# An attention and expert-FFN kernel: the work between the first attention and the expert gather is redistributed over the engines, and the expert loop is written out with its row scaling on VectorE alone

## What is computed

```
x = x + L0_xattn(layernorm(x), ctx, ctx)            # 32 heads of 8
h = layernorm(x)                                    # L0 experts: 8 experts, top 2
logits = h @ router_w.T; top 2 of softmax, renormalised
expert(h) = down( up(h) * square(relu(gate(h))) )   # every linear is "bitlinear":
  bitlinear(a, w): a rounded to 127 steps of its row maximum, w to {-1,0,1} of its mean
x = x + sum over the two experts of weight * expert(h)
x = x + L1_xattn(layernorm(x), ctx)                 # 16 heads, rope, latent keys
x = x + L1_ffn(layernorm(x))                        # top 1 of 32 masked ternary matrices
```

## Time and profile before

| what | value |
|---|---|
| median of 3 runs | 449.67 us (447.81 to 506.16) |
| the profiled execution's own time | 448.24 us |
| its span, first to last instruction | 446.1 us, mean granted clock 0.941 |
| busy: PE, DVE, ACT, POOL | 82%, 75%, 48%, 29% of the span |
| share of the chain that ended last: PE, ACT, DVE, issue, DMA | 58%, 14%, 11%, 8%, 5% |

### The profile page before, as it was taken

How to read it: one execution, slowest core, us unless ns; L and a number is a source line. 1 busy time by engine, 2 the same in 40 slices (tenths; PEclk the granted TensorE clock), 3 DMA queues, 4 the chain that set the end, 5 groups by cost and what they waited for, 6 DMA issues and landing times.

```text
span 446.1 us, 10544 instructions
## 1 busy us (share of the span) xinstructions
PE 367.6 (82%) x3670; PEld 254.5 (57%) x3677; DVE 332.6 (75%) x848; ACT 213.0 (48%) x467; POOL 129.9 (29%) x137
## 2 busy tenths in 40 slices
PE   2678878814777779998999999999999989638995
PEld 1466667712444446765457566475574778525884
DVE  6969999897888888598588777886876535673453
ACT  3799998261688888673013121231232221225441
POOL 1110000205466653111293141350430410153334
PEclk9999999755799999999999999999999999858999
DMA  8996850511265551441112112032031101343001
GB/s 289 411 395 241 316 199 3 190 41 38 33 243 174 166 153 50 143 175 40 45 51 95 25 73 95 1 95 95 1 96 53 44 1 60 130 108 94 18 32 37
DMA packets 17182, 50.76 MB, mean 114 GB/s; under 512 B 2104, under 2 KB 6464, under 8 KB 15088
## 3 DMA queue, kind: packets, MB, share of 16 engines
q1 hardware_dynamic: 14272, 42.46, 26.4%
q0 software_dynamic: 2864, 7.68, 5.9%
HBM read 43.44 MB, written 6.69 MB: 112 GB/s over the span
## 4 chain that ended last, share of the span: by engine, by line
PE 58%; ACT 14%; DVE 11%; issue 8%; DMA 5%; SPq 1%; POOL 1%; ACTq 0%; DVEq 0%; POOLq 0%
PE bank L956 17%; PE bank L1170 8%; PE bank L972 6%; PE bank L1044 5%; ACT W L1203 4%; DMA raw<-in_L_ffn_w_dram 3%; PE bank L983 3%; PE bank L815 3%; PE bank L826 2%; PE bank L997 2%; ACT hid L1294 2%; PE bank L833 2%; PE bank L1023 2%; ACT pnat L1189 2%; PE bank L1007 2%
## 5 line engine op out<-in xcount | busy, mean ns | idle before, releaser
L1734 DVE TENSOR_TENSOR roped<-bank,cst 128x512 f32<-128x512 f32 x96 | 61.1, 685 | 29.0 <-PE bank L956 28.0
L608 POOL TENSOR_TENSOR WE<-WE,wT 128x512 f32<-128x512 f32 x32 | 42.2, 1347 | 82.1 <-DMA WE<-_L_ffn_expert_masks_dram 82.1
L956 PE MATMUL bank<-XNT_hi,AW_hi 128*128 128x512 f32 x96 | 41.8, 435 | 0.5 <-DVE XNT_lo L1786 0.5
L1339 ACT ACTIVATE qrT<-bank 128x512 f32<-128x512 f32 x16 | 8.7, 595 | 62.2 <-PE bank L983 62.2
L956 PE MATMUL bank<-XNT_lo,AW_hi 128*128 128x512 f32 x96 | 37.8, 393 | 0.0
L956 PE MATMUL bank<-XNT_hi,AW_lo 128*128 128x512 f32 x96 | 37.6, 391 | 0.0
L1333 ACT ACTIVATE prob<-prob 128x512 f32<-128x512 f32 x16 | 10.1, 632 | 44.3 <-DVE prob L1744 44.3
L972 PE MATMUL bank<-roped,MW 128*64 128x512 f32 x128 | 31.0, 605 | 0.0
L1044 PE MATMUL bank<-VW,ctxT 128*128 128x256 f32 x128 | 30.7, 385 | 0.0
L580 POOL DMA_INDIRECT xg<-x_rows,owner_b x23 | 22.3, 971 | 28.1 <-DVE owner_b L428 14.2
L956 PEld LDWEIGHTS bank<-XNT_hi,AW_hi 128*128 128x128 f32 x96 | 18.0, 187 | 19.9 <-issue 11.4
(11 more groups left out here) (306 smaller groups left out, 874.8 us busy)
## 6 DMA issues: line engine op xcount, KB each, us to landing
raw<-in_L_ffn_w_dram SPq DMA_DIRECT2D x8, 1536.0 KB, 7.8
fold<-in_L_xattn_fold_dram SPq DMA_DIRECT2D x8, 1024.0 KB, 5.9
WE<-_L_ffn_expert_masks_dram SPq DMA_DIRECT2D x8, 1024.0 KB, 5.4
kv<-in_keys_values_dram SPq DMA_DIRECT2D x8, 656.0 KB, 7.6
yg<-y_rows SPq DMA_DIRECT2D x8, 256.0 KB, 4.7
x_tok<-pay SPq DMA_DIRECT2D x8, 256.0 KB, 2.2
X<-in_x_dram SPq DMA_DIRECT2D x4, 256.0 KB, 9.6
x_rows<-xrow SPq DMA_DIRECT2D x1, 516.0 KB, 4.3
```

The source lines that it names most:

```text
L608: pool.tensor_tensor(WE[:, e], WE[:, e], wT[:], ALU.mult).then_inc(WE_ready, 1)
L956: mm = pe.matmul(bank[g][:], a[:, k, c * P:(c + 1) * P], b[:, k, g * 512:(g + 1) * 512], start=k == 0 and i == 0, stop=k == 1 and i == 2)
L1734: ins = dve.tensor_tensor(roped[n][:, r, :].rearrange("p (b s) -> p b s", s=S), src, cst[:, None, at:at + S].to_broadcast([P, 8, S]), ALU. ...
```

## The change

Two groups of edits, both ahead of 182 us. Nothing of stage 4 changes but the semaphore counts that it waits for.

Routing chain. The inverse root goes to POOL as one power; each tile's mean is aggregated as the tile comes (`mean_ready`), and POOL centres rows 0 to 6 into XC during the attention. Row maxima are taken of XC (`row_peaks`) and scaled by the inverse root afterwards. ACT quantises tiles 0 to 3 and POOL tiles 4 to 7, and `xrow` is stored in two halves. The router's statistics and its turning move into the attention (tile 5 and tile 7). The last two tiles are turned singly (`turn_late_x1`), the logits of seven tiles are copied ahead of the last tile's, and ahead of the keys. `at_row` becomes 16 narrow instructions on a bf16 iota; the multiplications of `of_block` go to POOL (tile) and ACT (row).

Expert loop. PE's and DVE's loops are written out. `gate_up` runs four blocks ahead instead of three, `down` one block later. DVE scales every block; ACT no longer scales hidden rows but makes the output scale of each block (`output_scale`, formerly L1667 on DVE).

```diff
-            link(dve.tensor_tensor(R.of_block[:, 0], blk[...], cst[...], ALU.is_equal))
-            for k in range(R.choices):
-                dve.tensor_tensor(R.of_block[:, 1, c], R.of_block[:, 0, c], cst[:, C_TILE...], ALU.mult)
-            dve.tensor_scalar(R.of_block[:, 2], R.of_block[:, 0], cst[:, C_ROW:C_ROW + 1], None, ALU.mult)
-            for k in range(R.choices):
-                dve.tensor_tensor(R.at_row[:, c], lo[:, c, None]..., cst[:, None, C_IOTA...], ALU.is_equal).then_inc(spots_ready, 1)
+            dve.tensor_tensor(R.of_block[:, 0], blk[...], cst[...], ALU.is_equal).then_inc(of_block_ready, 1)
+            for c in range(n):
+                dve.tensor_scalar(R.at_row[:, c], iota_b[:], lo[:, c:c + 1], None, ALU.is_equal).then_inc(spots_ready, 1)
...
 # POOL
-            link(pool.tensor_scalar(less_mean[:], mv[:, :, 0], -1.0, 0.0, ALU.mult, ALU.add))
-            for t in range(NT // 2, NT):
-                pool.tensor_scalar(XN[:, t, :], X[:, t, :], less_mean[:, t:t + 1], rstd[:, t:t + 1], ALU.add, ALU.mult).then_inc(XN_pooled, 1)
-            pool.wait_ge(xrow_stored, 16)
+            for t in range(NT - 1):
+                pool.wait_ge(mean_ready, t + 1)
+                pool.tensor_scalar(XC[:, t, :], X[:, t, :], mv[:, t, 0:1], 1.0, ALU.subtract, ALU.mult).then_inc(rows_pooled, 1)
+            pool.wait_ge(var_ready, 2)
+            pool.tensor_tensor(rstd[:], var[:], minus_half[:], ALU.pow).then_inc(root_ready, 1)
+            pool.wait_ge(xs_ready, 1)
+            for t in range(NT // 2, NT):
+                pool.tensor_scalar(xq32[:, t, :], XC[:, t, :], xs[:, t:t + 1], MAGIC, ALU.mult, ALU.add).then_inc(rows_pooled, 1)
+            pool.wait_ge(of_block_ready, 1)
+            for k in range(2):
+                ins = pool.tensor_tensor(RB.of_block[:, 1, c], RB.of_block[:, 0, c], cst[:, C_TILE...], ALU.mult)
+            ins.then_inc(of_tile_ready, 1)
+            pool.wait_ge(xrow_stored, 32)
...
 # PE, routing
+            turn_x1(2)
             weigh(NT - 1)
+            pe.wait_ge(r_ready, 1)
+            router_logits([0])
             turn_outputs(NT - 1)
-            for h in range(3):
-                router_logits(h)
-            turn_x1(3)
-            router_logits(3)
+            router_logits([1])
+            turn_late_x1(NT - 2)
+            router_logits([2, 3])
+            turn_late_x1(NT - 1)
+            router_logits([4, 5, 6]).then_inc(logits_ready, 1)
+            router_logits([7]).then_inc(logits_ready, 1)
...
 # PE, experts
+            gate_up(3, expert_at(3))
+            for j in range(NBLK):
...
+                turn_hidden(j)
+                if j + 4 < NBLK:
+                    turn_rows(j + 4)
+                if j:
+                    down(j - 1, expert_at(j - 1))
+                if j + 4 < NBLK:
+                    gate_up(j + 4, expert_at(j + 4))
...
 # ACT, experts
                 hidden_rows(j, j % 2)
...
-                if j + 3 < NBLK:
-                    relus(j + 3, (j + 3) % 2)
-                if j % 2 == 0 and j + 1 < NBLK:
-                    scale_hidden(j + 1)
-                outputs(j)
+                output_scale(j)
+                if j:
+                    outputs(j - 1)
+                if j + 4 < NBLK:
+                    relus(j + 4, j % 2)
...
 # DVE, attention and routing
-                if t == NT - 2:
+                link.after(measured)
+                dve.bn_aggr(mv[:, t - 1, :], stats[:, t - 1, :]).then_inc(mean_ready, 1)
+                if t == NT - 3:
                     dve.wait_ge(r_loaded, 16)
                     link(dve.bn_stats(r_stats[:], r_raw[:]))
...
             dve.wait_ge(logits_copied, 1)
+            tops(range(NT - 1))
+            peaks = link.note(dve.tensor_reduce(row_max[:, 3, NT - 1:], XC[:, NT - 1:], AX.X, ALU.max, apply_absolute_value=True))
+            dve.wait_ge(logits_copied, 2)
+            topped = tops([NT - 1])
+            dve.wait_ge(root_ready, 2)
+            scaled = link.note(dve.tensor_tensor(row_max[:, 0, :], row_max[:, 3, :], rstd[:], ALU.mult))
+            top_indices([0, 1])
+            scale = link.note(dve.tensor_scalar(row_max[:, 0, :], row_max[:, 0, :], EPS, 1.0 / QMAX, ALU.max, ALU.mult))
...
 # DVE, experts: one block
+                if j:
+                    scale = link.note(dve.tensor_scalar(was[:, 2:3], was[:, 1:2], was[:, 0:1], EPS, ALU.mult, ALU.max))
+                gated = link.note(dve.scalar_tensor_tensor(h[:], bank[2 - par][:], 0.0, relu[par][:], ALU.max, ALU.mult))
+                inverse = link.note(dve.reciprocal(was[:, 3:4], was[:, 2:3]))
+                dve.tensor_tensor(h[:], h[:], bank[4 - par][:], ALU.mult).then_inc(hid_done, 1)
+                factor = link.note(dve.tensor_scalar(was[:, 4:5], was[:, 3:4], was[:, 0:1], QMAX, ALU.mult, ALU.mult))
+                highest = link.note(dve.tensor_reduce(hs[j % 4][:, 1:2], h[:], AX.X, ALU.max, apply_absolute_value=True))
+                dve.tensor_scalar(hid[(j - 1) % 4][:], hid[(j - 1) % 4][:], was[:, 4:5], MAGIC, ALU.mult, ALU.add).then_inc(hid_scaled, 1)
```

More of the change, by code:

```diff
@@ L912, in _ @@
                     fold_keys(0)
[L913 removed]
+                elif j == NBLK - 1:
                     fold_queries(1, 1)
[L915 removed]
+            down(NBLK - 1, expert_at(NBLK - 1))
             pe.sem_inc(keyed, 2)
@@ L1605, in _ @@
-            dve.wait_ge(logits_copied, 1)
-            best(dve, link, RB)
+            dve.wait_ge(x1_ready, NT)
+            measured = link.note(dve.bn_stats(stats[:, NT - 1, :], X[:, NT - 1, :]))
+            row_peaks(1, 2)
+            link.after(measured)
+            link(dve.bn_aggr(mv[:, NT - 1, :], stats[:, NT - 1, :]))
+            dve.tensor_scalar(var[:], mv[:, :, 1], EPS, None, ALU.add).then_inc(var_ready, 1)
+            last_row = link.note(dve.tensor_scalar(XC[:, NT - 1, :], X[:, NT - 1, :], mv[:, NT - 1, 0:1], None, ALU.subtract))
@@ new lines, in _, with tops, top_indices @@
+            row_peaks(2, NT - 1)
+            def tops(tiles):
+                for t in tiles:
+                    ins = dve.max(RB.top[:, t, :], RB.logits[:, t, :])
+                return link.note(ins)
+            def top_indices(tiles):
+                for t in tiles:
+                    ins = dve.max_index(RB.top_i[:, t, :], RB.top[:, t, :], RB.logits[:, t, :])
+                return link.note(ins)
+            dve.wait_ge(logits_copied, 1)
+            tops(range(NT - 1))
+            link.after(last_row)
@@ L1671, in scale_even @@
-            def scale_even(j, r):
-                dve.wait_ge(h_scale_ready, j + 1)
-                dve.tensor_scalar(hid[r][:], hid[r][:], hs[r][:, 4:5], MAGIC, ALU.mult, ALU.add).then_inc(hid_scaled, 1)
-            def hidden(j, r):
-                par = r % 2
-                first = isinstance(j, int) and j == 0
-                if not isinstance(j, int) or j >= 4:
+            for j in range(NBLK):
+                h, par = hid[j % 4], j % 2
+                was = hs[(j - 1) % 4]
+                if j:
+                    link.after(highest)
+                    scale = link.note(dve.tensor_scalar(was[:, 2:3], was[:, 1:2], was[:, 0:1], EPS, ALU.mult, ALU.max))
+                if j >= 4:
@@ L1680, in hidden @@
                     dve.wait_ge(h_turned, j - 1)
                 dve.wait_ge(relu_ready, j + 1)
-                gated = link.note(dve.scalar_tensor_tensor(hid[r][:], bank[2 - par][:], 0.0, relu[par][:], ALU.max, ALU.mult))
-                if not first:
-                    scale = row_scale((r + 3) % 4)
+                gated = link.note(dve.scalar_tensor_tensor(h[:], bank[2 - par][:], 0.0, relu[par][:], ALU.max, ALU.mult))
+                if j:
+                    link.after(scale)
+                    inverse = link.note(dve.reciprocal(was[:, 3:4], was[:, 2:3]))
@@ L1709, in _ @@
+            dve.tensor_scalar(hid[(NBLK - 1) % 4][:], hid[(NBLK - 1) % 4][:], was[:, 4:5], MAGIC, ALU.mult, ALU.add).then_inc(hid_scaled, 1)
             dve.sem_inc(roped_ready, 2)
```

317 lines of the change are left out of this document (154 added, 163 removed).

## The result

The changed kernel takes **447.89 us** (median) where the kernel before takes 449.99 in the same jobs: ratio **0.9942**, 95% interval 0.9924 to 0.9960: 2.1 us by the medians, 2.6 by the ratio, which leaves out one slow execution of each kernel (506.16 and 1204.66 us). The forecast was 441.7, in a range from 436.8 to 447.0; the result lies 0.9 us above its upper end. The two profiles stand against each other by distances, because the stretch ahead of the attention's first result varies by itself: that row begins between 32.4 and 35.1 us in the profiles of this study.

What follows compares the result with a forecast made beforehand. Bounds: DVE's dependent chain up to the owners and the expert loop's period. Savings of 4.6 and 2.3 us, 6.9 off the profiled 448.24, gave 441.3, expected as a measured 441.7 us; range 436.8 to 447, 8 in 10.

Steps and rivals of the forecast that it cites:

- The chain up to the owners: DVE's dependent stretch up to the owner list, with the attention ahead of it: 4.6 us saved (−0.5 + 4.0 + 1.1).
- Attention: Before X is complete: router statistics one tile earlier delay the score maxima, +0.5 us (bounds −0.4 and +0.9).
- X to the one-hots: Last tile of X to the one-hots: 11.49 us becomes 7.5, saving 4.0 (bounds 3.4 and 5.5).
- rival (a): PE keeps 2.4 GHz through the router and DVE's 2.57 us sets the loop: 438.0 us; chance 0.17.
- One-hots to owners: One-hots to the owner list, 8.17 us before: saving 1.1 us (bounds −0.5 and 1.9).
- The harsher rule: At `at_row`: DVE two-port and POOL instructions exclude each other entirely, making the total 0.8 us later; not adopted.
- the 0.26 of the copy: One-hots to owners: the copy of the counts goes from DVE, saving 0.26 us.
- the loop's ring: Expert loop: `turn_hidden`, ACT's two copies, `gate_up`, next `turn_hidden` form a dependent cycle of 2.70 us per block.
- rival (c): PE's sequencer takes the expert's number behind the wait for copied rows; decides from 0.4 us per block, 450.7 us; chance 0.07.
- the 18 turns: Expert loop from `turn_hidden(0)`, 8.0 us after the first gated row: 18 rings of 2.70 us, 48.6 in all.
- The tail: Behind the last gated row: PE has one `turn_hidden` and one `down` more to do, about 1.0 us.
- (b): POOL's descriptor writing waits for DVE's scaling and bounds the loop: 443.9 us, at worst 448.2; chance 0.18.

Runs made afterwards that it cites:

- loop_alone: The kernel before with only the changed expert loop (written out, all scaling on DVE, `down` a block behind); 452.79 us, ratio 1.0050.
- rows_ahead: The changed kernel with gathered rows turned ahead of `turn_hidden` on PE and copied ahead of the hidden row on ACT; 439.82 us, ratio 0.9782.
- words_ahead: The changed kernel with all five packed words loaded into PE's registers before the loop; 448.25 us, ratio 0.9965.
- fixed_experts: The changed kernel with experts set to block number modulo 8 from the fourth block on, for timing only; 444.85 us, ratio 0.9852.
- stats_first: rows_ahead with the router's statistics taken in DVE's idle time in the second tile; 438.95 us, ratio 0.9743.
- three_ahead: The changed kernel with `gate_up` three blocks ahead and `down` in the same block, still written out; 439.63 us, ratio 0.9788.
- chain_alone: The changed kernel's chain up to the owners with the expert loop of before put back; 446.40 us, ratio 0.9913.

## Why the prediction was wrong

**The chain up to the owners came out right**: 4.93 us against 4.6. Its parts did not, so the agreement is partly luck: 0.56 worse, 1.5 better and 0.6 worse. *Attention*: +1.06 against +0.5, but 0.26 of that is the later start and 0.2 a longer third step, which `loop_alone` shows as well; the change costs 0.6, namely 0.8 at tile 5, 0.72 of it the statistics, less 0.2 by which the last two steps are shorter; what gives that back no run took apart. *X to the one-hots*: 5.5 saved against 4.0. I priced the router at 1.2 GHz; it ran at 2.4, so DVE and not the logits came last. This is the first half of rival (a). It is not always so: in four of the twelve profiles with the new chain (`rows_ahead`, `words_ahead`, `fixed_experts`, `stats_first`) the clock fell within 0.6 us of X, DVE waited 0.3 to 0.5 us for the logits, and the stretch took 6.3 to 6.6 us in place of 6.0. *One-hots to owners*: 0.5 against 1.1. The narrow instructions were priced well, 0.16 us each against 0.155, and the contention with POOL did fall on them: 0.6 us where I put 0.4. The harsher rule that the prediction quotes fits better than the part of an instruction that I took: during POOL's two products, 0.95 us, DVE ended two instructions in place of six, each 0.05 us behind a product. What I had not priced is contention ahead of them: the two gate rows took 0.38 and 0.41 us beside POOL's rounding of `xq`, where the next row of that shape takes 0.15, and that ate the 0.26 of the copy.

**The step that failed is the loop's ring, "0.70 + 0.58 + 0.38 + 0.13 + 0.91 = 2.70 us".** The ring was there, and four terms were right (0.70, 0.57, 0.39, 0.87). The 0.13 is 0.33, and the load of a word puts 0.25 more on the 0.91 in every fourth block: fifteen turns at the high clock took 43.05 us, 2.87 each, 2.6 us over the forecast. It is rival (c), at a price below the 0.4 from which it was to decide, and I gave it 0.07 by the argument that "the same shifts stood in the loop before". They did, but there they ran while PE was still busy with `turn_hidden`. In the kernel before, in the turn in which `turn_hidden`'s four matmuls run from 136.63 to 137.29 us, the records for `gate_up` up to 137.2 are:

```profile
L815 PEldq ALU_OP  x2: 36/36/36, 136.9 to 137.0; - x2
L815 PEldq FUSED_REGOPS  x2: 46/46/46, 137.1 to 137.2; - x2
```

In a ring the same work lies on the path. And the 0.13 could not show it: the `gate_up` from which I read it, at 110.31, is block 1's, whose expert is loaded plain and needs neither shift nor mask.

The other half of the miss is the first three of the 18 turns. I let all of them run at 2.4 GHz from 8.0 us after the first gated row (`turn_hidden(0)` came at 8.06). They took 3.97, 3.69 and 3.13, 2.7 us over, since the clock was at 1.2 GHz until 120.4 us, 7.3 after `turn_hidden(0)`. With 0.35 at the end, 2.6 + 2.7 + 0.35 is the 5.7 by which the loop's 65.7 exceeds the forecast's 60.0. The tail was right: from the last gated row to the end of the last `down` 8.83 − 7.60 = 1.23 against 1.0.

**The rivals.** (b) fell: POOL's issues stayed at medians of 0.97 and 0.99 us with a scaling in every block. The second half of (a), DVE's 2.57 as the loop's bound, is what `rows_ahead` and `three_ahead` reach, with POOL's 2.56 beside it. What the experiments show of the gain that was expected of the loop: it was there, 6.6 us from `chain_alone` to `rows_ahead`, and taking `gate_up` four blocks ahead on rows copied in the same block turned it into a loss.

What stays open is why the ring keeps TensorE at 1.2 GHz longer in most executions: no run changed that alone.

## What to carry to other kernels

Before work is taken further ahead, list what its last operand waits for: a product four blocks ahead whose rows are copied in the same block is in a ring, and every short step of the sequencer behind that wait is paid each turn. Work that was hidden behind other work has no price in the old trace, so give it a price of its own when it moves behind a wait, and read that price where the same work is done. And read the next bound before moving work between engines: here POOL's issue rate stood just behind the ring, so where the scaling ran did not matter.

## What the runs showed of the hardware

- A two-input DVE instruction on SBUF and a POOL instruction that reads SBUF hold each other up: POOL's 128x184 product took 0.49 us beside narrow one-input instructions and 1.44 beside the wide `tensor_tensor`, whose pair took 2.65 in place of 2.35. The Trainium skill, SBUF — State Buffer, "Who interferes with whom", says that a DVE instruction with two SBUF inputs contends with a GpSimd instruction that reads SBUF. By that these rows agree. The other case in that page of the Trainium skill, a DVE instruction in a two-port mode that starves POOL's descriptors, showed nowhere here: POOL's issues kept 0.97 and 0.99 us with a scaling in every block.
- A narrow DVE instruction with one tensor as input can be held up by POOL as well: `at_row` took 0.55 and 0.53 us beside POOL's products and 0.24 otherwise.
- POOL's indirect transfers, a gather and a scatter in turn, come one per 1.27 to 1.29 us at best (0.97 to 0.99, and 0.30 behind each); the shortest step between any two, from one gather to the next, is 1.25.
- On PE the register work for a weights' address, behind a wait, holds the first matmul up by some 0.1 us for each operation, 0.28 in all for shift, mask and address.
